# Result rows behind the next step's masks, z in two rooms, the projection split around the first value group, x1's transposes later

## The reference

```python
q = rmsnorm(rope(h @ Wq_c @ Wq_up))          # 16 heads of 128
k_sw, v_sw = rmsnorm(rope(h @ Wk)), h @ Wv   # one shared key/value head
ck = rmsnorm(h.reshape(b, t // 16, 16 * 256) @ W_comp)   # one key per 16 tokens
c_out  = attend(q . ck * scale,  block ended before the token, sink, values ck)
sw_out = attend(50 * tanh(q . k_sw * scale / 50),  last 64 tokens, sink, values v_sw)
ao = c_out + sw_out
x  = layernorm(h + (ao grouped @ Wg) @ Wo)
x  = layernorm(x + x @ w_ternary.T + bias)
```

## Time and profile before

| what | value |
|---|---|
| time, median of 3 runs | 428.15 us (423.61 to 428.4) |
| profiled execution, its own time | 426.38 us |
| its span | 424.6 us |
| busy in the span: PE, DVE | 367.8 us (87%), 326.7 us (77%) |
| busy in the span: ACT, POOL | 287.3 us (68%), 302.3 us (71%) |
| mean DMA share over the span | 62.4% of 16 engines (queue 1) |
| mean granted clock of TensorE | 0.965 |

### The profile page before, as it was taken

The page is one execution under the profiler, slowest core; times in us unless marked ns, Lnnn a source line. Parts: engine busy times, 40 slices in busy tenths (PEclk is TensorE's granted clock), DMA queues, the critical chain, the costliest instruction groups (busy, mean ns, idle before and its releaser), DMA issues.

```text
span 424.6 us, 8753 instructions
## 1 busy us (share of the span) xinstructions
PE 367.8 (87%) x3109; PEld 297.5 (70%) x3111; DVE 326.7 (77%) x663; ACT 287.3 (68%) x818; POOL 302.3 (71%) x190
## 2 busy tenths in 40 slices
PE   5995798959979998999999999888889999989781
PEld 5993586656757767787878687767676877768660
DVE  2685789677888889897979787989886998963311
ACT  4557775767695969687777767686967695956200
POOL 1834361266796979798989777897979697986805
PEclk9998899978999999999999999999998999999995
DMA  7994004688756676767567676777676676584330
GB/s 248 316 247 112 1 0 67 233 247 124 124 91 123 100 138 95 130 101 121 106 112 103 107 110 108 114 110 139 97 127 100 115 100 125 87 137 76 47 66 25
DMA packets 150284, 50.20 MB, mean 118 GB/s; under 512 B 138593, under 2 KB 148833, under 8 KB 149985
## 3 DMA queue, kind: packets, MB, share of 16 engines
q1 hardware_dynamic: 149424, 49.32, 62.4%
q10 hardware_dynamic: 816, 0.33, 0.3%
HBM read 11.87 MB, written 4.19 MB: 38 GB/s over the span
## 4 chain that ended last, share of the span: by engine, by line
PE 33%; issue 17%; POOL 17%; DVE 11%; ACT 9%; DMA 7%; SPq 6%; POOLq 0%; ACTq 0%; DVEq 0%
PE PS L664 10%; POOL ao L1196 5%; PE PS L615 5%; POOL room_wg L1206 4%; SPq L373 4%; PE PS L641 3%; ACT room_h L822 3%; DMA aoT<-ao 3%; PE PS L471 3%; PE PS L633 3%; ACT ao L704 3%; PE PS L431 2%; PE PS L581 2%; DVE room_K L1112 2%; DMA room_h<-room_K 2%
## 5 line engine op out<-in xcount | busy, mean ns | idle before, releaser
L1196 POOL TENSOR_TENSOR ao<-room_wg,ao 128x1024 f16<-128x1024 f32 x32 | 68.2, 2132 | 28.0 <-ACT ao L704 27.9
L664 PE MATMUL PS<-V,room_wg 128*128 128x129 f32 x512 | 67.0, 285 | 13.7 <-POOL room_wg L1206 10.2
L664 PEld LDWEIGHTS PS<-V,room_wg 128*128 128x128 f32 x512 | 63.3, 197 | 18.8 <-POOL room_wg L1206 13.5
L1206 POOL TENSOR_TENSOR room_wg<-room_comp,keep 128x1024 f32<-128x1024 f32 x32 | 74.7, 2355 | 1.4 <-ACT room_comp L813 1.4
L822 ACT ACTIVATE room_h<-PS,room_K 128x8 f32<-128x8 f32 (+7 forms) x256 | 70.7, 364 | 1.9 <-DVE room_K L1047 1.7
L822 ACT ACTIVATION_READ_ACCUMULATOR room_h<-PS,room_K 128x1 f32 x256 | 62.4, 250 | 0.0
L633 PE MATMUL PS<-Weff,aoT 128*128 128x256 f16 x512 | 58.5, 273 | 3.8 <-DMA aoT<-ao 3.7
L1212 POOL TENSOR_TENSOR ny<-nx,nu 128x16 f32<-128x16 f32 x16 | 46.8, 2924 | 18.3 <-DVE nx L1023 18.3
L633 PEld LDWEIGHTS PS<-Weff,aoT 128*128 128x128 f16 x512 | 49.6, 98 | 10.8 <-issue 4.8
L1021 DVE TENSOR_REDUCE ssq<-room_wg 128x8 f32<-128x1024 f32 x30 | 36.5, 1220 | 21.9 <-ACT room_wg L773 21.5
L581 PE MATMUL PS<-room_h,kT 128*128 128x512 f16 x192 | 47.9, 391 | 4.2 <-ACT room_comp L809 2.4
(11 more groups left out here) (178 smaller groups left out, 734.5 us busy)
## 6 DMA issues: line engine op xcount, KB each, us to landing
H<-in_L_attn_h SPq DMA_DIRECT2D x4, 512.0 KB, 6.3
room_wg<-in_L_attn_Wg SPq DMA_DIRECT2D x1, 2048.0 KB, 14.7
cw_rows<-staged SPq DMA_DIRECT2D x1, 2048.0 KB, 6.4
CW<-cw_rows SPq DMA_DIRECT2D x1, 2048.0 KB, 7.9
aoT<-ao SPq DMA_TRANSPOSE x128, 2.7
out<-room_wo SPq DMA_DIRECT2D x16, 128.0 KB, 2.0
CW<-in_L_attn_Wq_up SPq DMA_DIRECT2D x2, 512.0 KB, 13.5
room_wo<-in_L_attn_Wo SPq DMA_DIRECT2D x1, 1024.0 KB, 15.2
```

The source lines that it names most:

```text
L664: last = nc.tensor.matmul(pv, Pm[:, c, 2 * pr:2 * pr + 2, :], V[:, 2 * i + c, :], start=True, stop=True)
L1196: G.tensor_tensor(ao16[:, 1, c, :, :], ao[:, c, :, :], ao16[:, 0, c, :, :], ALU.subtract).then_inc(g_al, 1)
L1206: G.tensor_tensor(Pm[:, c, :, :], E[:, c, :, :], keep[:, :, :], ALU.mult).then_inc(g_mask, 1)
```

## The change

z gets a second room, and the result rows of a tile are written one step later. In step i (3 to 15) POOL writes the rows of tile i-3 right after both masks; in step 16 those of tile 13 come first and those of tile 14 last, in step 17 those of tile 15. SP's stores follow the same list (`stored`). DVE's z waits for the rows of tile i-4 instead of i-3, and the aggregation of the second norm's statistics waits for the rows of tile i-3, since these still read mv.

The projection in a middle step now begins with the fp32 blocks, goes on with the first 16 - 2g heads of the high part, and leaves 2g heads for after values(0), ahead of the low part, which now ends the sum.

PE's two transposes of x1 move from ahead of the scores to behind their second group; ACT's copy of x1T's high part moves from ahead of square(1) to behind the first tanh.

```diff
--- before.py
+++ after.py
@@ -85,7 +85,8 @@
         staged = sb("staged", [P, HEADS, HID])
         CW = sb("CW", [P, CHUNKS, HID])
         wqc2 = over("wqc2", [P, 2, KC, 2, QC], f32r)
-        wfT = sb("wfT", [P, 2, KC, HID], f16)[:, 0, :, :]
+        room_f = sb("room_f", [P, 2, KC, HID], f16)
+        wfT = room_f[:, 0, :, :]
         fb_s = sb("fb_s", [P, HID])
         sinkb = sb("sinkb", [P, HEADS])
         e0, e1w, skp, skm = (sb(n, [P, HEADS]) for n in ("e0", "e1w", "skp", "skm"))
@@ -149,6 +150,7 @@
         below = room_h[:, 2560:3072].bitcast(bf16).rearrange("p (a n) -> p a n", n=NBLK)
 
         y, z, x1, res = (room_wo[:, HID * n:HID * (n + 1)] for n in range(4))
+        zs = z, room_f[:, 1, :, :].rearrange("p k n -> p (k n)").bitcast(f32)
         PcT = part(room_wo, 1024, "p (a q) -> p a q", TPB * P, q=P)
         ssk = sb("ssk", [P, NT + 1])
         ssq = sb("ssq", [P, HEADS])
@@ -330,6 +332,10 @@
 
         PARTS = ((0, 0), (1, 0), (0, 1))
 
+        def stored(i):
+
+            return [i - 3] if 3 <= i < NT else [NT - 3, NT - 2] if i == NT else [NT - 1] if i > NT else []
+
         def all_steps(body):
 
             for i in range(-1, NT + 2):
@@ -386,9 +392,9 @@
                     queries(i + 1)
                 if 0 <= i < NT:
                     outputs(i)
-                if i >= 2:
-                    sp.wait_ge(g_out, i - 1)
-                    sp.dma_start(out_v[(i - 2) * P:(i - 1) * P, :], res[:, :]).then_inc(s_out, 16)
+                for tile in stored(i):
+                    sp.wait_ge(g_out, tile + 1)
+                    sp.dma_start(out_v[tile * P:(tile + 1) * P, :], res[:, :]).then_inc(s_out, 16)
             sp.wait_ge(s_out, 16 * NT + 16)
 
 
@@ -544,7 +550,8 @@
                     t = i + 1
                     if t:
                         queries(t)
-                if ffn:
+
+                def norm_T():
                     pe.wait_ge(g_x1, i - 1)
                     wait(pe, d_fr, i - 2)
                     if not mid:
@@ -563,6 +570,7 @@
                     last.then_inc(p_f, 1)
 
                 if ffn and not mid:
+                    norm_T()
                     feed_forward()
                 if i == 0:
                     pe.wait_ge(s_lo, 9)
@@ -582,6 +590,8 @@
                                                     qT[:, qp, 8 * hf:8 * hf + 8, c * WIN:(c + 1) * WIN],
                                                     start=n == 0, stop=n == 2)
                         last.then_inc(p_sw, 1)
+                        if ffn and u == 1:
+                            norm_T()
 
                     first, n = (i // TPB) * NBLK, SUB * groups(i)
                     for hf in range(2):
@@ -603,50 +613,42 @@
                     output_weights()
                 o = bank(7)[:, 0:HID]
 
-                def project_blocks(start, chunks):
-
-                    if 0 in chunks:
-                        pe.wait_ge(a_ct, t + 1)
-                        if t == 0:
-                            pe.wait_ge(s_cwr, 16)
-                    end, last = groups(t) - 1, None
-                    for g in chunks:
-                        rows = P - HEADS if g == end else P
-                        last = nc.tensor.matmul(o, PcT[0:rows, g, :], CW[0:rows, TPB * (t // TPB) + g, :],
-                                                start=start and g == 0, stop=not start and g == end)
-                    return last
+                def project_blocks():
+
+                    pe.wait_ge(a_ct, t + 1)
+                    if t == 0:
+                        pe.wait_ge(s_cwr, 16)
+                    for g in range(groups(t)):
+                        rows = P - HEADS if g == groups(t) - 1 else P
+                        nc.tensor.matmul(o, PcT[0:rows, g, :], CW[0:rows, TPB * (t // TPB) + g, :],
+                                         start=g == 0, stop=False)
+
+                def project_high(heads):
+
+                    for hd in heads:
+                        if hd == 0:
+                            pe.wait_ge(s_ah, 64 * t + 64)
+                        for wp in range(2):
+                            nc.tensor.matmul(o, aoT[:, 0, hd % 2, hd // 2, :], Weff[:, wp, hd, :],
+                                             start=False, stop=False)
+
+                def project_low():
+
+                    pe.wait_ge(s_al, 64 * t + 64)
+                    for hd in range(HEADS):
+                        last = nc.tensor.matmul(o, aoT[:, 1, hd % 2, hd // 2, :], Weff[:, 0, hd, :],
+                                                start=False, stop=hd == HEADS - 1)
+                    last.then_inc(p_o, 1)
 
                 if proj:
 
                     t = i - 1
+                    ahead = HEADS - 2 * groups(t) if mid else HEADS
                     if i == 1:
                         copied(pe, G_FT)
                     wait(pe, d_y, t)
-                    if not mid:
-                        project_blocks(True, range(groups(t)))
-                    pe.wait_ge(s_ah, 64 * t + 64)
-
-                def project_high():
-
-                    for hd in range(HEADS):
-                        for wp in range(2):
-                            last = nc.tensor.matmul(o, aoT[:, 0, hd % 2, hd // 2, :], Weff[:, wp, hd, :],
-                                                    start=mid and hd == wp == 0, stop=False)
-                    return last
-
-                def project_low():
-
-                    pe.wait_ge(s_al, 64 * t + 64)
-                    for hd in range(HEADS):
-                        last = nc.tensor.matmul(o, aoT[:, 1, hd % 2, hd // 2, :], Weff[:, 0, hd, :],
-                                                start=False, stop=not mid and hd == HEADS - 1)
-                    return last
-
-                if proj and mid:
-                    project_high()
-                elif proj:
-                    project_high()
-                    project_low().then_inc(p_o, 1)
+                    project_blocks()
+                    project_high(range(ahead))
 
                 def values(c):
 
@@ -669,9 +671,9 @@
                     values(0)
                 if i == -1:
                     value_weights()
-                if proj and mid:
+                if proj:
+                    project_high(range(ahead, HEADS))
                     project_low()
-                    project_blocks(False, range(groups(t))).then_inc(p_o, 1)
                 if mid:
                     values(1)
 
@@ -789,13 +791,18 @@
                         query_high(0, g - 4)
 
             def step(i, front, mid, proj, ffn):
+
+                def feed_forward_high():
+
+                    act.wait_ge(p_xt, i - 1)
+                    narrow(x1T[:, 0, :, :], x1_bank(mid).rearrange("p (k n) -> p k n", k=KC), a_xt)
+
                 if front and i < 1:
                     square(i + 1, 0)
-                if ffn:
-                    act.wait_ge(p_xt, i - 1)
-                    narrow(x1T[:, 0, :, :], x1_bank(mid).rearrange("p (k n) -> p k n", k=KC), a_xt)
                 if front:
                     square(i + 1, 1)
+                if ffn and not mid:
+                    feed_forward_high()
                 if i == -1:
                     output_weights()
                 if i == 0:
@@ -808,6 +815,8 @@
                         act.wait_ge(p_sw, 4 * i + u + 1)
                         nc.scalar.activation(E[:, c, 8 * hf:8 * hf + 8, :], bank(b).rearrange("p (a q) -> p a q", q=WIN),
                                              ACT.Tanh, scale=1.0 / CAP).then_inc(a_tanh, 1)
+                        if ffn and u == 0:
+                            feed_forward_high()
                     for c in range(2):
                         act.wait_ge(a_tanh, 4 * i + 2 * c + 2)
                         nc.scalar.activation(E[:, c, :, :], E[:, c, :, :], ACT.Exp, scale=CAP).then_inc(a_es, 1)
@@ -1051,11 +1060,11 @@
                 if ffn:
                     dve.wait_ge(p_f, i - 1)
                     dve.wait_ge(g_xb, i - 1)
-                    wait(dve, g_out, i - 2)
-                    V_.scalar_tensor_tensor(z[:, :], ffn_bank(mid), fscale[:, 0:1], x1b, ALU.mult,
+                    wait(dve, g_out, i - 3)
+                    V_.scalar_tensor_tensor(zs[i % 2], ffn_bank(mid), fscale[:, 0:1], x1b, ALU.mult,
                                             ALU.add).then_inc(d_fr, 1)
                     dve.wait_ge(d_fr, i - 1)
-                    chained(V_.bn_stats(bns[:, 1, :], z[:, :]))
+                    chained(V_.bn_stats(bns[:, 1, :], zs[i % 2]))
                 if first:
                     weights_rest(1)
                 if front:
@@ -1130,6 +1139,8 @@
                 if proj or ffn:
                     after_link()
                     sets = slice(0 if proj else 1, 2 if ffn else 1)
+                    if ffn:
+                        wait(dve, g_out, i - 2)
                     for n in range(sets.start, sets.stop):
```

(35 more changed lines are left out.)

## The result

The changed kernel takes **417.96 us**, median of 6 runs (415.7 to 420.05), against 427.28 for the kernel before on the same chips. The ratio is 0.9846, interval 0.9804 to 0.9887: faster by 1.5%. The interval excludes no change, and it excludes a gain of 2% too. The forecast was 420, and 8 us less than before in the profiled execution; that execution now takes 418.8 us (426.38 before), its span 417.0 (424.6).

What follows compares the result with a forecast made beforehand. No engine was saturated; three loops within 0.9 us bounded each cycle. Taking the least gain over 13 cycles gave 8.0 us, so 428.15 - 8 = 420 us, range 415 to 428.5.

Steps and rivals of the forecast that it cites:

- three loops: GpSimd's, VectorE's and PE's sequences in each step, within 0.9 us of each other; a cycle gains the least of the three.
- Part 1: Result rows moved behind the masks: the pow waits for nx alone and starts 0.90 us earlier a cycle.
- loop G: GpSimd's pow, two masks, then values(0): gains 0.90 us a cycle at most, 10.8 in 12.
- The store wait: GpSimd at the result rows behind the masks stalls about 0.8 us, hidden; as slower rival about 431 us, chance 0.07.
- Part 2: Projection split around values(0): blocks fill the wait for ao's high parts, gaining about 1.3 us at step 11, 0.8 at step 2.
- The equal exchange: Ahead of values(0), fp32 passes of 0.45g us replace fp16 matmuls of 0.46g; time there and the sum stay the same.
- two waits: PE's waits for ao's high parts at steps 11 and 2, gains of about 1.3 and 0.8 us.
- a possible loss at the low parts: After values(0) at g 1 and 2, PE might wait up to 0.8 us more for low parts; costed at nothing.
- Part 3: x1's transposes and ScalarE's copy later: scores no longer wait for x1 (3.7 us), square(1) comes 0.26 us earlier.
- loop V: VectorE's rope, maximum, z, normalisation and division: gains 0.37 us a cycle plus removed waits, ceiling 11.5 in 12 cycles.
- The sum: Least of the loops' gains over 13 cycles: 8.0 us in total; step 15 may lose 0.1, the tail nothing.
- The port: VectorE's first division instructions beside the result rows: each meeting holds VectorE 1.21 us, giving 436 us; chance 0.07.

Runs made afterwards that it cites:

- e8: The whole change plus one more GpSimd instruction of the result rows' size (1.22 us) right ahead of the pow in steps 3 to 14; 0.9916 of before.
- e6: The whole change with two rooms for the result rows and a semaphore for each, so rows never wait for the store just issued; 0.9844 of before.
- e10: The whole change with all 16 heads of the high part ahead of values(0), behind the blocks; 1.0043 of before.
- e11: The whole change with the fp32 blocks back at the end of the sum, 2g heads of the high part staying behind values(0); 1.0498 of before.
- e4: The kernel before with the moved result rows and the later x1 transposes, without the projection's split; 0.9962 of before.
- e5: The whole change with x1's transposes and ScalarE's copy of x1T back ahead of the scores and of square(1); 0.9897 of before.
- e9: e7 with VectorE's nx of the layer norms made by a reduction instead of a tensor_scalar; 0.9828 of before.
- e7: The whole change plus one more GpSimd instruction of the result rows' size (1.22 us) behind the masks in steps 3 to 15; 0.989 of before.

## Why the prediction was right, point by point

The mechanism came as forecast: the pow follows nx, PE's waits for masks, x1 and the high parts went, and three loops close together. That the number fits as well as it does is in part luck, as the point on the sum shows.

- **Part 1.** The pow follows nx as forecast, 0.90 a cycle for loop G. e8 confirms what the old place costs in ordinary cycles (0.6 to 1.0 in columns 2, 3 and 8 to 11) and corrects the total: 5.9 us in all, not 10.8, since it costs 0.4 at most in columns 4 to 7 and 13, which are bound elsewhere. The prediction had capped such cycles as well.
- **The store wait.** Forecast at 0.8 us in step 9, measured 0.65 and 8.1 in all. A sign that the prediction had named for being wrong, GpSimd idle over 1 us before the result rows on a DMA, did come: 1.82, 1.04 and 1.70 us in the twelve cycles and 2.00 in step 15. e6 shows that it was hidden nevertheless. The time given for this rival, 431, does not follow from its own terms: 0.6 us lost in each of 13 steps is 436.
- **Part 2.** The equal exchange is right, and e10 and e11 show how much hangs on it. Its worth is the term that was mis-sized: I had two waits, 1.3 and 0.8 us, "both inside the sums below", and a possible loss at the low parts. e4 against the whole change gives 4.6 us from first to last mask, and 0.9962 against 0.9846, intervals apart. The 4.6 us stand in columns 2 to 4, 11 and 12. There e4 waits 3.5 us for high parts, 1.0 for low ones, and also 2.0 for queries in step 4, so not all of the 4.6 need be the split's.
- **Part 3.** 0.26 for square(1) and 0.11 for nx are there. I had loop V gain 0.37 a cycle; of this part 3's share is 0.26, and e5 against the whole change gives 0.2 in ordinary ones.
- **The sum.** The twelve cycles gave 9.3 us, and with the one into step 2, as the prediction counts them, 10.6 where it had 8.0. Most of the excess is the cycle into step 12, 2.6 instead of 0.3: before's wait for queries was not there. The wait for ScalarE's exps stands in the values(0) of step 7, so it acts on the cycle into step 8, not into step 7 as the sum had it: into step 8 there were 0.34 instead of 0.9 (the exps came 0.96 us late for the last value matmuls), into step 7 nothing instead of 0.3. What brought 10.6 back to the 7.6 us between the spans was costed at nothing or nearly: the cycle into step 15, 0.9 us longer instead of 0.1 (the scores of step 15 wait 1.63 us for their queries and have the transposes in their middle), 1.5 us ahead of the first mask, which the change does not touch, and 0.6 behind the last, less than the profiles differ there among themselves (40.0 to 41.7 us in all but e10 and e11). The errors cancel, and this is luck.
- **The port.** I gave it 0.07 on the strength of nx beside the result rows, which took 0.29 instead of 0.18. That was one pair of instructions, and it holds for that pair in all twelve steps of before (0.29 to 0.32 us). VectorE's nx of the layer norms, beside GpSimd's subtraction, is held to its end, and so is the first nx in e9. The rival's place was wrong (not the division's first instructions), its mechanism exists: 1.2 us in the whole change.

## What to carry to other kernels

When several loops close within a microsecond, cost an edit against each of them and take the least; an edit that does nothing alone (part 3) or half (part 1) can be worth it in company. Keep the work ahead of a synchronising point equal to the time its operand needs: swap pieces there instead of moving them, and put what needs no DMA first. A slower stage moved into idle time still decides what stands beside it.

## What the runs showed of the hardware

A tensor_scalar of VectorE on 128x2 fp32 in SBUF, issued while GpSimd subtracts 128x1024, ended with it, up to 2.14 us instead of 0.17 (e7); a reduction of the same values took 0.16 at all times (e9). Beside GpSimd's tensor_scalar of 128x256 (1.22 us) another VectorE tensor_scalar (128x16) was not held to the end, only 0.29 to 0.32 instead of 0.17, in twelve steps of before. The same instruction beside the subtraction was held to its end, five times in e9, up to 1.08 us. What it is in GpSimd's instruction that decides, its operation, its number of inputs or its length, was not tried.
